# Head-wise keys spread by ScalarE and VectorE instead of by DMA, and values by half tiles, in a three-attention vision tower on one Trainium2 core

## The chip, the cores and the metric

One Trainium2 chip (trn2), one of its cores. The metric is the time of one execution on the device in microseconds, start to end. A run of the kernel is timed several times; the kernel before took 1170.06 us in the median of three runs (1166.44 to 1171.95).

## The reference

64 images of 96x96x3 are cut into 36 patches of 768 values each (2304 tokens in all) and embedded into 192 columns. Then come, all in float32:

```python
# attn1: causal attention, 12 heads of 64 columns, residual, layer norm
# attn2: attention, 12 heads of 16 columns, layer norm before it (two sizes by image),
#        no mask, no bias on q, k, v; then an MLP of 768 with gelu, mixed by gumbel weights
# attn3: attention, 12 heads of 16 columns, bias on q, k, v, ALiBi distance bias,
#        residual, layer norm after it
# moe:   top-2 of 8 experts and a shared expert of 768 columns
a = jax.nn.softmax(jnp.einsum('bhnd,bhmd->bhnm', q, k) * scale, axis=-1)
o = jnp.einsum('bhnm,bhmd->bhnd', a, v)
```

## The kernel before

The tokens stand as 18 tiles of 128 tokens. The stages run one after another: embed, `wide_stage` (attn1), `narrow_stage` (attn2), `mlp_stage`, `narrow_stage` again (attn3), `moe_stage`. Each engine has its own program, written out in order by hand, and semaphores join them; there is no planner. Between stages all engines meet at a barrier.

**Both attention stages** work in 8 groups of 288 tokens (8 images). A group has 4 units of 2 images (72 tokens), and the loop over `k` makes one step a unit, `j = k % 4`. In step k TensorE does `scores(k)`, `turn(k-2)` (transposes of the probabilities), a share of the projections for the *next* group g, `project_out` for the tiles that are ready (18 tiles in 32 units), and `mix(k-2)` (probabilities by values). Every float32 product with a weight is five matmuls of split operands (lines 286 to 290, 779 to 783). The projections of a group go to PSUM banks 0 and 1 in turn, and a bank can be written again only after what is in it has been copied out.

**wide_stage (attn1).** Twelve chunks of 128 columns a group: six of queries, then six of keys, alternating banks (`bank(c % 2)`); four of them in each of the steps j = 0, 1, 2. ScalarE copies the queries (`copy_q`, L400) and the lower half of each key chunk (`copy_k_low`, L409), VectorE the upper half (`copy_k_high`, L492), behind its `sum_up` and `take_scores` in the step. In step j = 3 come the values of the group's 2 or 3 tiles: each tile fills bank 0 and bank 1 with 384 columns each (L304 to L308), and one ScalarE copy of 768 columns (L418) empties both; the next tile's first matmul waits for it, as do the transposes of the next group's tokens (L271).

**narrow_stage (attn2, attn3).** Per group there are three chunks: c = 0 holds the queries of heads 0 to 7, c = 1 their keys, c = 2 the queries (partitions 0 to 63) and keys (64 to 127) of heads 8 to 11. The scores of all heads come out of one matmul because the keys stand block-diagonally: `keys_a[p][16h:16h+16, h, :]` has head h's keys, all else is zero (cleared once by POOL, L730). ScalarE copies c = 0, 1, 2 to `q_a`, `k_a`, `qk_b` (L911 in attn2, L913 with a bias in attn3), and SP's queue spreads them by 8 DMAs (`spread_keys_a`, L653) and 4 DMAs (`spread_keys_b`, L659) of 18 KB each:

```python
for h in range(8):
    sp.dma_start(keys_a[g % 2][16 * h:16 * h + 16, h, :], k_a[16 * h:16 * h + 16, :])
```

Step j = 0 transposes the group's tokens, j = 1 projects c = 0 and 1, j = 2 projects c = 2 and the first third of the values, j = 3 the other two thirds; `spread_values` (9 DMAs, L673) follows on SP. `scores` of a group's first unit waits for all 12 key DMAs. ScalarE's order in a step is `exponentiate(k-1)`, `copy_turned(k-2)`, the projection copies, `copy_z(k-2)`; VectorE's is `sum_up(k-1)`, `take_scores(k)`, then the norm's work and the residual. POOL raises to a power, shifts and normalises, and at the stage's start clears the key and value buffers. In attn3 SP, ScalarE and POOL also bring in and split the weights of the last stage (`side`: `load_step` after each `spread_values`, `load_down` once at k = 6, after `spread_keys_b(2)`).

Of the kernel before, what the change touches and what calls it, by code (L numbers as in the profile page):

```python
# [10 lines left out]
ALU = mybir.AluOpType  # L11
# [123 lines left out]
def wide_stage(nc, psum, ident, neg_half, name, h_tok, w_q, w_k, w_v, w_o, bias, q_bias, k_bias, out_bias):  # L135
# [30 lines left out]
    with Sems(nc, name) as S, ExitStack() as ctx:  # L166
# [41 lines left out]
        def _(sp):  # L208
            for t in range(NT):
                sp.wait_ge(S["v_copied"], t + 1)  # L210
# [55 lines left out]
        def _(pe):  # L266
            def transpose_x(g):
                if g > 0:
                    pe.wait_ge(S["v_copied"], tiles_upto(g - 1))
# [5 lines left out]
            def project(g, c):  # L275
                if c < 2:
                    pe.wait_ge(S["x_split"], g + 1)
                elif c < chunks + 2:
                    pe.wait_ge(S["q_copied"], chunks * g + c - 1)
                else:  # L280
                    pe.wait_ge(S["k_low_copied"], chunks * g + c - chunks - 1)
                    pe.wait_ge(S["k_high_copied"], chunks * g + c - chunks - 1)
                w, n = (w_q, c) if c < chunks else (w_k, c - chunks)
                cols, toks = slice(n * P, (n + 1) * P), group_cols(g)
                out = bank(c % 2)[:, 0:WIDE]
# [5 lines left out]
                                 ).then_inc(S["qk_done"], 1)  # L291

            def values(t):
                g = min(o for o in range(groups) if t < tiles_upto(o))
                if t == new_tiles(g)[0]:
                    pe.wait_ge(S["k_low_copied"], chunks * (g + 1))
                    pe.wait_ge(S["k_high_copied"], chunks * (g + 1))
                else:
                    pe.wait_ge(S["v_copied"], t)
                at = (t % RING) * P  # L300
                toks = slice(at, at + P)
                for b in range(2):
                    cols, out = slice(b * 384, (b + 1) * 384), bank(b)[:, 0:384]
# [4 lines left out]
                    last = nc.tensor.matmul(out, b_x[:, toks], w_v.b_lo[:, cols], start=False, stop=True)  # L308
                last.then_inc(S["v_done"], 1)
# [51 lines left out]
            for c in range(2 * chunks):  # L361
                project(0, c)
# [4 lines left out]
            for k in range(steps):  # L367
# [5 lines left out]
                if g < groups:  # L373
                    if j < 3:
                        for c in range(4 * j, 4 * j + 4):
                            project(g, c)
# [11 lines left out]
        def _(act):  # L388
# [7 lines left out]
            def copy_q(g, c):  # L396
                act.wait_ge(S["qk_done"], 2 * chunks * g + c + 1)
                if g >= 2:
                    act.wait_ge(S["scores_done"], per_group * (g - 1))
                nc.scalar.activation(q[g % 2][:, c, 0:WIDE], bank(c % 2)[:, 0:WIDE], ACT.Identity,  # L400
                                     bias=q_bias[:, c:c + 1], scale=1 / 8).then_inc(S["q_copied"], 1)

            def copy_k_low(g, n):
                act.wait_ge(S["qk_done"], 2 * chunks * g + chunks + n + 1)
# [45 lines left out]
            for n in range(chunks):  # L450
                copy_k_low(0, n)
# [1636 lines left out]
```

## Time and profile before

| | |
|---|---|
| median of three runs | 1170.06 us |
| the profiled execution | 1165.79 us, of which the span is 1164.0 us |
| busy: TensorE 1013.6, weight loads 925.2, VectorE 561.9, ScalarE 395.4, POOL 319.6 us | 87, 79, 48, 34, 27% of the span |
| attn1, from 56.8 to 328.2 us | 271.4 us |
| attn2, from 328.2 to 496.8 us | 168.6 us |
| attn3, from 631.1 to 804.5 us | 173.4 us |

The profile names instructions by line and engine: PE is TensorE's matmuls and PEld its weight loads, DVE is VectorE, ACT ScalarE, SPq the DMA queue of SyncE. A number behind an x counts instructions. In square brackets or behind a second bar stands the idle time of that engine just before, and what ended it; "issue" there means that the profile shows nothing that it waited for.

### The profile page before, as it was taken

How to read it: one execution, taken by the hardware profiler on the slowest of the kernel's cores; microseconds unless marked ns; L12 is line 12 of the kernel's file. 1: busy time of each engine (PE TensorE's matmuls, PEld its weight loads, DVE VectorE, ACT ScalarE, POOL GpSimd, SP SyncE). 2: the span in 40 equal slices, each digit the busy share in tenths (PEclk: the TensorE clock that was granted, in tenths of full speed). 3: DMA queues.
4: the chain of work that ended last, by engine and by line, in shares of the span. 5: the costliest groups of instructions: out<-in, count | busy, mean ns of one | idle time of the engine just before them, and what ended most of it. 6: DMA issues, size and time to landing. Idle time of an engine off the chain costs nothing. (4 is left out here: it accounts for less than half of the span.)

```text
span 1164.0 us, 21593 instructions
## 1 busy us (share of the span) xinstructions
PE 1013.6 (87%) x8306; PEld 925.2 (79%) x8306; DVE 561.9 (48%) x1489; ACT 395.4 (34%) x882; POOL 319.6 (27%) x349
## 2 busy tenths in 40 slices
PE   6879998999847999868998678976999999999997
PEld 6768888888735777758997466865999999999996
DVE  2225454555544666457331355654444454545444
ACT  1245554555413455323442344542212121111110
POOL 4424343443441222224223465663000000000000
PEclk9999999999977899879998898986999999999999
DMA  9711010101001111000000142210000000000000
GB/s 294 219 39 24 24 33 24 33 23 29 29 4 27 26 29 28 16 1 1 1 1 22 48 115 66 65 47 3 1 1 12 1 11 1 11 1 12 1 11 11
DMA packets 40757, 39.08 MB, mean 34 GB/s; under 512 B 21072, under 2 KB 32208, under 8 KB 40656
## 3 DMA queue, kind: packets, MB, share of 16 engines
q1 hardware_dynamic: 38528, 33.38, 10.3%
q10 hardware_dynamic: 2128, 4.34, 1.3%
q8 instruction: 66, 1.08, 0.4%
q14 instruction: 35, 0.29, 0.1%
HBM read 21.76 MB, written 1.77 MB: 20 GB/s over the span
## 5 line engine op out<-in xcount | busy, mean ns | idle before, releaser
L1485 ACT ACTIVATE moe_silu<-psum 128x384 f32<-128x384 f32 x108 | 53.2, 492 | 273.7 <-PE psum L76 266.3
L1389 POOL TENSOR_TENSOR moe_rstd<-moe_var_eps,neg_half 128x3 f32<-128x3 f32 x6 | 5.1, 851 | 349.5 <-DVE moe_var_eps L1584 349.5
L715 POOL TENSOR_TENSOR attn_prob<-attn_prob,attn_recip 100x432 f32<-100x432 f32 x64 | 58.3, 912 | 132.2 <-DVE attn_recip L1036 132.2
L839 PEld LDWEIGHTS psum<-attn_prob_t,attn_values 108*64 108x64 f32 x1024 | 66.6, 214 | 24.5 <-issue 10.5
L839 PE MATMUL psum<-attn_prob_t,attn_values 108*64 108x36 f32 x1024 | 74.1, 293 | 10.5 <-DMA attn_values<-attn_v_tok 6.2
L1555 DVE TENSOR_TENSOR moe_hid_pair<-psum,moe_silu 128x384 f32<-128x384 f32 x72 | 40.1, 557 | 87.3 <-PE psum L76 87.3
L813 PE MATMUL psum<-attn_keys_a,attn_q_a 128*64 128x288 f32 x256 | 51.2, 480 | 35.4 <-issue 23.2
L1571 DVE SCALAR_TENSOR_TENSOR moe_acc<-psum,moe_coef,moe_acc 128x192 f32<-128x192 f32 x144 | 59.7, 418 | 44.9 <-PE psum L1439 44.5
L1439 PE MATMUL psum<-w_dn,moe_hid_pair 128*128 128x192 f32 x288 | 73.4, 337 | 6.3 <-DVE moe_acc L1571 6.3
L72 PE MATMUL psum<-moe_x_a_hi,w_gu_a_hi 128*128 128x384 f32 x216 | 76.2, 353 | 0.0
L235 POOL TENSOR_TENSOR attn_prob_x<-attn_prob,attn_recip 100x864 f32<-100x864 f32 x32 | 52.6, 1643 | 76.4 <-DVE attn_recip L517 76.4
L74 PE MATMUL psum<-moe_x_a_hi,w_gu_a_lo 128*128 128x384 f32 x216 | 72.9, 338 | 0.0
L73 PE MATMUL psum<-moe_x_a_lo,w_gu_a_hi 128*128 128x384 f32 x216 | 72.9, 338 | 0.0
L76 PE MATMUL psum<-moe_x_b,w_gu_b_lo 128*128 128x384 f32 x216 | 72.9, 337 | 0.0
L75 PE MATMUL psum<-moe_x_b,w_gu_b_hi 128*128 128x384 f32 x216 | 72.8, 337 | 0.0
L1031 DVE TENSOR_REDUCE attn_row_sum<-attn_prob 100x12 f32<-100x432 f32 x64 | 38.5, 602 | 63.2 <-ACT attn_prob L927 62.9
L1439 PE MATMUL psum<-w_dn_mid,moe_hid_pair 128*128 128x192 f32 x288 | 69.0, 335 | 0.0
L1236 ACT ACTIVATE mlp_hid<-psum,columns 128x384 f32<-128x384 f32 x72 | 39.9, 581 | 54.2 <-PE psum L76 36.3
L1439 PEld LDWEIGHTS psum<-w_dn,moe_hid_pair 128*128 128x128 f32 x288 | 49.0, 190 | 10.9 <-DVE moe_acc L1571 10.7
L1439 PEld LDWEIGHTS psum<-w_dn_mid,moe_hid_pair 128*128 128x128 f32 x288 | 47.0, 189 | 4.9 <-DVE moe_acc L1571 3.7
L1726 PE MATMUL psum<-embed_w_tok,embed_patches 128*128 128x192 f32 x216 | 39.5, 341 | 10.3 <-DMA embed_w_tok<-in_tok_w 5.8
L1726 PEld LDWEIGHTS psum<-embed_w_tok,embed_patches 128*128 128x128 f32 x216 | 36.4, 197 | 13.1 <-DMA embed_patches<-in_x 7.2
(318 smaller groups left out, 2698.3 us busy)
## 6 DMA issues: line engine op xcount, KB each, us to landing
embed_patches<-in_x SPq DMA_DIRECT2D x18, 384.0 KB, 23.1
attn_v<-attn_v_tok SPq DMA_DIRECT2D x16, 216.0 KB
attn_values<-attn_v_tok SPq DMA_DIRECT2D x96, 27.0 KB
attn_keys_a<-attn_k_a SPq DMA_DIRECT2D x128, 18.0 KB, 1.8
raw_a<-in_w_gu_dram SPq DMA_DIRECT2D x8, 288.0 KB, 3.2
raw_b<-in_w_gu_dram SPq DMA_DIRECT2D x16, 144.0 KB, 3.2
y<-moe_y SPq DMA_DIRECT2D x6, 288.0 KB
attn_keys_b<-attn_qk_b SPq DMA_DIRECT2D x64, 18.0 KB, 1.8
```

The costliest lines, as they stand in the source:

```text
L72: nc.tensor.matmul(out, w.a_hi[:, cols], x.a_hi[:, toks], start=True, stop=False)
L73: nc.tensor.matmul(out, w.a_hi[:, cols], x.a_lo[:, toks], start=False, stop=False)
L74: nc.tensor.matmul(out, w.a_lo[:, cols], x.a_hi[:, toks], start=False, stop=False)
L75: nc.tensor.matmul(out, w.b_hi[:, cols], x.b[:, toks], start=False, stop=False)
L76: return nc.tensor.matmul(out, w.b_lo[:, cols], x.b[:, toks], start=False, stop=True)
L235: nc.gpsimd.tensor_tensor(prob_x[k % 2][:, :, :, :], prob[k % 3][:, :, :].rearrange("p h (a n) -> p h a n", a=1) .to_broadcast([QP, HEADS, ...
L715: nc.gpsimd.tensor_tensor(pr, pr, recip[k % 2][:, :].rearrange("p (h a) -> p h a", a=1) .to_broadcast([QP, HEADS, SEQ]), ALU.mult).then_in ...
L839: last = nc.tensor.matmul(ps[r:r + 64, n // 2, a * SEQ:(a + 1) * SEQ], v[:, n, :], prob_t[k % 2][:, n, a, :], start=True, stop=True)
L1439: last = nc.tensor.matmul(down_ps(n), hid(gr)[:, c, t * MT:(t + 1) * MT], w, start=(m == 0), stop=(m == len(terms) - 1))
L1485: nc.scalar.activation(silu[c % 2][:, :], bank(2 * (c % 2))[:, 0:MW], ACT.Silu).then_inc(S["silu_done"], 1)
L1571: ins = nc.vector.scalar_tensor_tensor(out=acc[:, t, :], in0=down_ps(n), scalar=scalar, in1=h_tok[:, 3 * i + t, :] if e == 0 else acc[:, t ...
L1726: last = nc.tensor.matmul(out_bank(t), patches[:, t, c, :], w_tok[:, c, :], start=(c == 0), stop=(c == chunks - 1))
```

## The change

It does four things. (1) attn1: values are handed over by half tiles: each bank has its own semaphore count and its own copy of 384 columns. (2) attn1: query and key chunks alternate, queries always in bank 0 and keys in bank 1, two pairs in each of j = 0, 1, 2; VectorE's copies follow, two in each of these steps instead of two in j = 1 and four in j = 2. (3) attn2, attn3: `spread_keys_a` and `spread_keys_b` and the buffer `k_a` are gone. ScalarE writes each head's keys straight from PSUM, eight copies of 128x288 scaled by a column of a 0/1 head mask, four behind `copy_z` in j = 1 and four in j = 2; VectorE writes the last four heads in one instruction in j = 2 (`mask_keys_b`). For the first group VectorE does both, the first as one instruction of 8x288 columns (`mask_keys_a0`). `keys_a` needs no clearing. (4) The first third of the values moves from j = 2 to j = 3 and waits for the eight masked copies, since they read bank 1. A head mask is made once at the start from the identity matrix, and a bias column by head for attn3.

```diff
@@ wide_stage, TensorE @@
-            def project(g, c):
-                if c < 2:
+            def project(g, kind, c):
+                if c == 0:
                     pe.wait_ge(S["x_split"], g + 1)
-                elif c < chunks + 2:
-                    pe.wait_ge(S["q_copied"], chunks * g + c - 1)
+                elif kind == 0:
+                    pe.wait_ge(S["q_copied"], chunks * g + c)
                 else:
-                    pe.wait_ge(S["k_low_copied"], chunks * g + c - chunks - 1)
-                    pe.wait_ge(S["k_high_copied"], chunks * g + c - chunks - 1)
+                    pe.wait_ge(S["k_low_copied"], chunks * g + c)
+                    pe.wait_ge(S["k_high_copied"], chunks * g + c)
+                out = bank(kind)[:, 0:WIDE]
...
                 for b in range(2):
+                    if t > new_tiles(g)[0]:
+                        pe.wait_ge(S["v_copied"], 2 * (t - 1) + b + 1)
+                    elif b == 0:
+                        pe.wait_ge(S["q_copied"], chunks * (g + 1))
+                    else:
+                        pe.wait_ge(S["k_low_copied"], chunks * (g + 1))
+                        pe.wait_ge(S["k_high_copied"], chunks * (g + 1))
...
@@ wide_stage, ScalarE and VectorE @@
+                for b in range(2):
+                    act.wait_ge(S["v_done"], 2 * t + b + 1)
+                    nc.scalar.activation(v_tok[t % vt_ring][:, b * 384:(b + 1) * 384], bank(b)[:, 0:384], ACT.Copy
+                                         ).then_inc(S["v_copied"], 1)
...
+                if g < groups and j < 3:
+                    copy_k_high(g, 2 * j)
+                    copy_k_high(g, 2 * j + 1)
@@ narrow_stage, SyncE @@
-            spread_keys_a(0)
-            spread_keys_b(0)
             spread_values(0)
...
-                if g < groups:
-                    if j == 1:
-                        spread_keys_a(g)
-                    if j == 2:
-                        spread_keys_b(g)
-                    if j == 3:
-                        spread_values(g)
+                if g < groups and j == 3:
+                    spread_values(g)
@@ narrow_stage, POOL @@
-                nc.gpsimd.memset(qk_b[p][:, WIDE:], 0.0).then_inc(S["pads_cleared"], 1)
+                nc.gpsimd.memset(q_b[p][:, :], 0.0).then_inc(S["pads_cleared"], 1)
             def clear(p):
-                nc.gpsimd.memset(keys_a[p][:, :, :], 0.0).then_inc(S["keys_cleared"], 1)
-                nc.gpsimd.memset(keys_b[p][:, :, :], 0.0).then_inc(S["keys_cleared"], 1)
+                nc.gpsimd.memset(keys_b[p][:, :, :], 0.0).then_inc(S["keys_b_cleared"], 1)
@@ narrow_stage, TensorE @@
             def values(g, n):
-                if n == 2:
-                    pe.wait_ge(S["v_copied"], 3 * g + 1)
-                else:
-                    pe.wait_ge(S["qk_copied"], 3 * g + 2 + n)
+                if n == 0:
+                    pe.wait_ge(S["keys_a_made"], 8 * g + 8)
+                elif n == 1:
+                    pe.wait_ge(S["q_b_copied"], g + 1)
+                    pe.wait_ge(S["keys_b_made"], g + 1)
+                else:
+                    pe.wait_ge(S["v_copied"], 3 * g + 1)
...
                         project(g, 2)
-                        values(g, 0)
                     else:
-                        values(g, 1)
-                        values(g, 2)
+                        for n in range(3):
+                            values(g, n)
@@ narrow_stage, ScalarE @@
+            def mask_keys_a(g, heads):
+                act.wait_ge(S["qk_done"], 3 * g + 2)
+                if g >= 2:
+                    act.wait_ge(S["scores_done"], per_group * (g - 1))
+                for h in heads:
+                    out, mask = keys_a[g % 2][:, h, :], head_mask[:, h:h + 1]
+                    if qk_bias is None:
+                        ins = nc.scalar.activation(out, bank(1)[:, 0:WIDE], ACT.Copy, scale=mask)
+                    else:
+                        ins = nc.scalar.activation(out, bank(1)[:, 0:WIDE], ACT.Identity,
+                                                   bias=k_bias_by_head[:, h:h + 1], scale=mask)
+                    ins.then_inc(S["keys_a_made"], 1)
...
                 if 2 <= k < units + 2:
                     copy_z(k - 2)
+                if g < groups and j == 1:
+                    mask_keys_a(g, range(4))
+                if g < groups and j == 2:
+                    mask_keys_a(g, range(4, 8))
@@ narrow_stage, VectorE @@
+            def spread_masked(out, keys, mask, bias):
+                both = [keys.rearrange("p (a n) -> p a n", a=1).to_broadcast(list(out.shape)),
+                        mask.rearrange("p (h a) -> p h a", a=1).to_broadcast(list(out.shape))]
+                if bias is None:
+                    return nc.vector.tensor_tensor(out, both[0], both[1], ALU.mult)
+                return nc.vector.scalar_tensor_tensor(out=out, in0=both[0], scalar=bias, in1=both[1],
+                                                      op0=ALU.add, op1=ALU.mult)
+
+            def mask_keys_a0():
+                dve.wait_ge(S["qk_done"], 2)
+                spread_masked(keys_a[0][:, :, :], bank(1)[:, 0:WIDE], head_mask[:, :],
+                              None if qk_bias is None else qk_bias[:, 1:2]).then_inc(S["keys_a_made"], 8)
...
             split_x(0)
+            mask_keys_a0()
+            mask_keys_b(0)
             if prenorm:
                 pre_stat(1)
                 pre_norm(1)
...
+                if j == 2 and g + 1 < groups:
+                    mask_keys_b(g + 1)
@@ prepare @@
-                    nc.vector.memset(c2_scale[0:DB, :], 0.25)
-                    nc.vector.memset(c2_scale[DB:P, :], 1.0)
-                    dve.wait_ge(S["const_ready"], 2)
+                    dve.wait_ge(S["const_ready"], 3)
+                    nc.vector.tensor_reduce(head_mask[:, :], ident[:, :].rearrange("p (h n) -> p h n", h=8),
+                                            axis=AX.X, op=ALU.add).then_inc(S["head_mask_ready"], 1)
```

## Rows read from the trace of the kernel before

**Rows 1.** Waits of PE in attn1 (56 to 327 us): total us, times, longest

```profile
PE psum L304 <- ACT attn_v_tok L418: 9.0, 10, 0.9
PE psum L286 <- DVE attn_k_diag L492: 6.4, 7, 1.1
PE psum L271 <- ACT attn_v_tok L418: 6.3, 7, 0.9
```

**Rows 2.** The same view in attn2 (327 to 496.5 us)

```profile
PE psum L813 <- issue: 7.8, 7, 1.9
```

**Rows 3.** The same view in attn3 (633 to 804 us)

```profile
PE psum L813 <- issue: 15.4, 7, 4.5
PE psum L839 <- DMA attn_values<-attn_v_tok: 6.2, 2, 5.6
PE psum L813 <- DMA attn_keys_b<-attn_qk_b: 5.9, 1, 5.9
```

**Rows 4.** ScalarE's groups of instructions in attn1: busy us, mean ns | idle before

```profile
L418 ACT ACTIVATE attn_v_tok<-psum 128x768 f32<-128x768 f32 x18 | 14.6, 810 | 32.8 <-PE psum L308 32.8
...
L393 ACT ACTIVATE attn_a_hi<-psum 128x384 fp32r<-128x384 f32 x2 | 1.0, 490 | 13.2 <-PE psum L272 13.2
```

**Rows 5.** Timeline of attn1, step j = 2: start us, duration us, engine line

```profile
221.15 0.37 PE L286 MATMUL psum<-attn_a_hi,w_k_a_hi 128*128 128x288 f32 x1 [0.88 <-DVE attn_k_diag L492]
```

**Rows 6.** Timeline of the start of attn2

```profile
332.34 5.04 DVE L998 TENSOR_SCALAR attn_x_hat<-h_tok,attn_pre_mv,attn_pre_rstd 128x192 f32<-128x192 f32 x3 [1.85 <-POOL attn_pre_rstd L704]
334.15 2.01 POOL L730 MEMSET attn_keys_a<- 128x2304 f32 x1
...
342.40 0.62 DVE L982 BATCH_NORM_STATS2 attn_pre_stats<-h_tok 128x6 f32<-128x192 f32 x2
344.33 2.12 DVE L998 TENSOR_SCALAR attn_x_hat<-h_tok,attn_pre_mv,attn_pre_rstd 128x192 f32<-128x192 f32 x2 [0.82 <-POOL attn_pre_rstd L704]
345.23 0.41 ACT L911 ACTIVATE attn_k_a<-psum 128x288 f32<-128x288 f32 x1 [0.79 <-PE psum L783]
...
354.63 1.23 PE L813 MATMUL psum<-attn_keys_a,attn_q_a 128*64 128x288 f32 x4 [6.33 <-DMA attn_keys_b<-attn_qk_b]
```

**Rows 7.** VectorE's one long operation with a broadcast operand, at the kernel's start

```profile
10.81 1.96 DVE L1734 TENSOR_TENSOR embed_pos<-embed_pos,embed_b_tok 128x1728 f32<-128x1728 f32 x1 [10.81 <-DMA embed_b_tok<-in_tok_b]
```

**Rows 8.** ScalarE's copies scaled by a column: ns min/median/max, first and last start

```profile
L911 ACT ACTIVATE attn_qk_b<-psum,c_scale x8: 500/501/501, 346.4 to 467.1; 128x288 f32<-128x288 f32 x8
L913 ACT ACTIVATE attn_qk_b<-psum,columns,c_scale x8: 583/590/593, 638.7 to 773.5; 128x288 f32<-128x288 f32 x8
```

**Rows 9.** Timeline of PE in attn3: the scores of four steps, two mixes

```profile
664.27 1.09 PE L813 MATMUL psum<-attn_keys_a,attn_q_a 128*64 128x288 f32 x4 [3.29 <-issue]
...
669.32 0.69 PE L813 MATMUL psum<-attn_keys_a,attn_q_a 128*64 128x288 f32 x4
...
672.99 0.69 PE L813 MATMUL psum<-attn_keys_a,attn_q_a 128*64 128x288 f32 x4
...
676.16 1.15 PE L839 MATMUL psum<-attn_prob_t,attn_values 108*64 108x36 f32 x16
677.13 0.69 PE L813 MATMUL psum<-attn_keys_a,attn_q_a 128*64 128x288 f32 x4
...
679.40 1.16 PE L839 MATMUL psum<-attn_prob_t,attn_values 108*64 108x36 f32 x16
```

**Rows 10.** Groups over the whole kernel: ScalarE's exponential and its copy of the transposes

```profile
L927 ACT ACTIVATE attn_prob<-attn_prob 100x432 f32<-100x432 f32 x64 | 35.7, 558 | 7.6 <-POOL attn_prob L722 7.5
...
L934 ACT ACTIVATE attn_prob_t<-psum 108x288 f32<-108x288 f32 x64 | 26.2, 409 | 58.4 <-PE psum L823 58.2
```

**Rows 11.** Timeline of SP's queue in attn3, the value DMAs of group 2

```profile
689.01 7.96 SPq L673 DMA_DIRECT2D attn_values<-attn_v_tok  x9
```

**Rows 12.** Windows without the stages' starts and ends: busy PE, PEld, DVE, ACT, POOL; clock

```profile
372.20:474.00 101.80, 94.38 (x936) 78.26 (x938) 63.31 (x159) 51.94 (x135) 25.45 (x29) 0.95 0.12 28
664.20:780.60 116.40, 98.65 (x936) 81.37 (x937) 69.65 (x176) 53.93 (x135) 69.53 (x79) 0.88 0.28 73
```

More of the change, by code:

```diff
@@ L307, in values @@
                     nc.tensor.matmul(out, b_x[:, toks], w_v.b_hi[:, cols], start=False, stop=False)
-                    last = nc.tensor.matmul(out, b_x[:, toks], w_v.b_lo[:, cols], start=False, stop=True)
-                last.then_inc(S["v_done"], 1)
+                    nc.tensor.matmul(out, b_x[:, toks], w_v.b_lo[:, cols], start=False, stop=True
+                                     ).then_inc(S["v_done"], 1)
             def scores(k):
@@ L360, in _ @@
             transpose_x(0)
-            for c in range(2 * chunks):
-                project(0, c)
+            for c in range(chunks):
+                project(0, 0, c)
+                project(0, 1, c)
             for t in new_tiles(0):
@@ L374, in _ @@
                     if j < 3:
-                        for c in range(4 * j, 4 * j + 4):
-                            project(g, c)
+                        for c in (2 * j, 2 * j + 1):
+                            project(g, 0, c)
+                            project(g, 1, c)
                     else:
@@ L449, in _ @@
                 copy_q(0, c)
-            for n in range(chunks):
-                copy_k_low(0, n)
+                copy_k_low(0, c)
             for t in new_tiles(0):
@@ L462, in _ @@
                     if j < 3:
-                        for c in range(4 * j, 4 * j + 4):
-                            if c < chunks:
-                                copy_q(g, c)
-                            else:
-                                copy_k_low(g, c - chunks)
+                        for c in (2 * j, 2 * j + 1):
+                            copy_q(g, c)
+                            copy_k_low(g, c)
                     else:
@@ L486, in copy_k_high @@
             def copy_k_high(g, n):
[L487 removed]
+                dve.wait_ge(S["k_done"], chunks * g + n + 1)
                 if g >= 2:
@@ L809, in scores @@
                 ps = scores_ps(k)
-                for q, keys, h0, h1 in ((q_a, keys_a, 0, 8), (qk_b, keys_b, 8, HEADS)):
+                for q, keys, h0, h1 in ((q_a, keys_a, 0, 8), (q_b, keys_b, 8, HEADS)):
                     for a in range(2):
@@ L949, in _ @@
             round_x(0)
-            for c in range(3):
-                copy_qk(0, c)
+            copy_q(0, 0)
+            copy_q(0, 2)
             for n in range(3):
```

112 lines of the change are left out of this document (43 added, 69 removed).

## The prediction

> **What bounds the kernel now.** I read the busy times first: TensorE is at 87% and every other engine below half, so what counts is where TensorE stands still, and I asked for its waits in each of the three attention stages. In attn1 [rows 1] the reader should see three regular waits: ten of 0.9 us for the copy of a value tile, seven of 0.9 us for the same copy ahead of the transposes, seven of about 0.9 us for VectorE's half of a key chunk. In attn2 and attn3 [rows 2, 3] the waits stand before `scores` (L813), once a group: 7.8 and 15.4 us in seven each. They are labelled "issue", but the first group of each stage waits at the same line for the last key DMA by name [rows 3, 6], and the seven are the seven other groups' first scores; I take them for the key DMAs too. One more wait, of 5.6 us, is for a group's values [rows 3]. Third, the windows: without starts and ends TensorE's granted clock is 0.95 in attn2 and 0.88 in attn3 [rows 12]. There are two levels, 1.2 and 2.4 GHz, so 0.95 means 0.10 x 101.8 = 10 us and 0.88 means 0.24 x 116.4 = 28 us at the lower one, 38 us in all.
>
> **The change part by part.**
>
> *Half tiles.* A tile's copy is 0.81 us for 768 columns, while 384 columns take 0.49 [rows 4]. Copying bank 0 now runs under the five matmuls into bank 1, which last longer than it does, so the ten waits go: -9.0. Ahead of the transposes the last half is still awaited, 0.81 - 0.49 = 0.32 shorter each, 7 x 0.32: -2.2.
>
> *Alternation.* The wait for VectorE [rows 5] falls once a group today, in j = 2, because two chunks are finished there before VectorE leaves `take_scores`. Afterwards the second key chunk of each of three steps waits for the first one's upper half. It comes third in the step, not second, so most of VectorE's delay has passed. Bounds: none (-6.4 in all) and a full 0.88 in each (7 x 3 x 0.88 = 18.5, so +12.1). I take 0.35 each, being two thirds of a microsecond later than the row's: 7 x 3 x 0.35 = 7.4 less 6.4: +1.0. attn1 together: -10.2.
>
> *Start of attn2.* POOL no longer clears `keys_a`, 2.0 us before its first power and 2.0 us behind it. The three scalings at 332.34 took 5.04 us [rows 6] and ended, at 337.38, as POOL's last memset of that run did; two such operations took 2.12 beside another memset. I read it as VectorE standing behind POOL: fewer memsets, an end 3.2 us earlier. If it were only slowed in proportion, the operations would start 1.3 us earlier and end so: -1.3, the term's other bound. The Trainium skill's page "SBUF — State Buffer", section "Who interferes with whom", states the first reading: one port pair is shared by the two engines as an exclusive lock, and the loser waits for the whole instruction.
>
> Next, the keys. The K chunk is ready at 345.2, the scores start at 354.6: 9.4 us [rows 6]. Instead VectorE writes 2304 columns. The nearest row is 1728 columns in 1.96 us [rows 7], 1.13 ns each: 2.6 us, and 1152 columns more are 1.4 (with the fixed part). The values then follow at half clock, some 2 us, for the banks are held by the masks. Scores at +5.9: 3.5 earlier. But group 1's statistics and scaling, which ran from 342.4 to 346.45 under cover [rows 6], now stand behind the masks, 4.0 us, and VectorE takes no scores before that: 345.2 + 4.0 + 4.0 = 353.2 against some 356.2 (scores 354.6 and their 1.6): 3.0 earlier. attn2's start: -6.2.
>
> *Start of attn3.* No norm there, so 3.5 of the 5.9 us [rows 3] go, less 0.5 since the 9 value DMAs (7.5 us of issue) then land late: -3.0.
>
> *Key waits, other groups.* The masked keys are there one step before the scores. -7.8 and -15.4 [rows 2, 3]: -23.2.
>
> *Values of group 2.* SP issues them at 689.01 [rows 11], behind key DMAs and ten loads of the down weights. With no key DMA between, those loads go out two steps earlier: -5.6.
>
> *What takes their place.* ScalarE gets eight copies a group. A copy scaled by a column is 0.50 us, with bias 0.59 [rows 8]; copies that follow each other overlap by some 0.1, so four are 1.6 in attn2, 2.0 in attn3. They stand behind `copy_z`, and behind them wait the exponential (0.56) and the copy of the transposes (0.41) [rows 10] that `mix` needs. From the end of one mix: `copy_z` and latency 0.3 (estimate), masks to 1.9 or 2.3, exponential and copy to about 2.85 or 3.25. Today a j = 2 step starts its mix 3.17 us after its scores (672.99 to 676.16 [rows 9]), with a tile of output projection (0.75, an estimate) and the first third of the values (0.47) in it; without the tile 2.4. Eighteen of 32 steps have a tile. So j = 2 costs on average nothing in attn2 and +0.4 in attn3. In j = 3, scores and transposes end 1.3 us after the mix (677.13 to 679.40 less two thirds of the values), and then the first third waits for the masks until 2.1 or 2.4: +0.8 or +1.1; its own 0.47 comes in; and the last third waits for the first one's copy behind the exponential: +0.25 to 0.4. Sum per group: 1.5 in attn2, 2.4 in attn3. Over seven groups each: 10.5 + 16.8 = +27.3. Bounds: masks at their full 0.50 and 0.59, with the overlap gone, raise it to about 38; masks that fit in today's gaps, ScalarE being busy only half of the time [rows 12], bring it to 6.6 (only the moved third of the values would show, 14 x 0.47).
>
> *VectorE's* 1.4 us for the last heads in j = 2 I cost at nothing: it is 63 us busy of 102 in attn2 [rows 12] and stands between `take_scores` and the next exponential. If that slack is gone it costs up to 1.4 x 14 = 20. The head mask at the start waits for an identity that POOL makes in the first microseconds, while VectorE stands idle for its first 10.81 us [rows 7]: nothing.
>
> *Clock.* The step from 664.27 to 669.32 took 5.05 us mostly at 1.2 GHz, the next, with more work, 3.67 [rows 9]: at least 0.27 us lost for each at that level, I take 0.3. Of the 38 us the waits of 3 to 5.6 us [rows 3] explain most, and those go; new ones of 1 us come. I give back a third: 38 x 0.3 / 3: -4.0. Bounds: +30 (below) and -11.4.
>
> **Sum:** -10.2 - 6.2 - 3.0 - 23.2 - 5.6 + 27.3 - 4.0 = -24.9. The profiled execution was 1165.79 with a span of 1164.0; it becomes 1140.9. It lies 4.3 below the median of the runs, 1170.06; against that median: **1145.2**. About 0.5% (5.9 us) is what a measurement of this kernel can tell from no change.
>
> **The rivals.**
>
> *attn1 gives nothing.* VectorE is late in all three steps (the +12.1 bound in place of +1.0), which eats the half tiles: 1145.2 + 11.1 = 1156. For it: VectorE leaves `take_scores` at about the same point of each step. Against: the second key chunk is one later.
>
> *ScalarE is the new pace.* Masked copies take 0.59 in both stages and do not overlap: four are 2.4, so +0.8 twice a group in attn2 and +0.4 in attn3, (1.6 + 0.8) x 7 = 17, and no clock comes back, +4: 1166. No change to speak of.
>
> *Slower: the clock falls in every group.* The long wait once a group is replaced by two or three short ones between short pieces of work, and TensorE runs at 1.2 GHz for half of each group. At 10 us in each of 14 groups it is 140 us at the lower level instead of the 25 that I expect: 115 x 0.3 = +35: 1180. It decides from about 126 us on, 9 a group (1145.2 + 101 x 0.3 = 1176). For it: the clock was down for 7 us in attn2 after waits of hardly 2 us in the longest [rows 2, 12]. Against: attn1, with waits of 0.9 us several times a group, shows no lowered clock in its steady part. The Trainium skill's page "TensorE: Matmul & The Clock Gate", section "What's actually happening", says that low is the default and activity lifts it, which would allow this.
>
> *It does not do what it says.* The waits labelled "issue" are not for keys and stay: 1145.2 + 23.2 = 1168. Against: they stand only before a group's first scores.
>
> **How the numbers follow.** Forecast 0.50, attn1 nothing 0.15, ScalarE's pace 0.16, slower 0.14, "issue" 0.05. Faster by over 0.5% are the first two and a part of the third: 0.70; within 0.5%: 0.16; slower: 0.14. The range reaches down to the forecast with the clock's whole 11.4 and no wait for VectorE (1145 - 7 - 7 = 1131) and up to the rivals at 1166 and 1168; 1168. The slower case stays out, and some of the gains beyond 1131.
>
> **What would show it.** attn1 shorter by about 10 us, no L304 wait for ScalarE, the VectorE wait three times a group at 0.3 to 0.4. attn2's first scores some 6 us earlier. No wait before `scores`; in its place one of about 1 us before the first third of the values, released by ScalarE's masked copies, and mix waiting for the copy of the transposes. SP's down loads two steps earlier and no 5.6 us wait. ScalarE's busy time up by 55 to 60 us, VectorE's by 27. A granted clock above 0.9 in both windows. I am wrong if masked copies are slower than 0.59, if the clock falls below 0.85 in the narrow stages, or if attn1 does not get shorter.

## The result, and the profile after the change

| | before | after |
|---|---|---|
| median of the runs | 1170.39 us (1166.44 to 1171.95, 4) | 1128.4 us (1125.69 to 1129.45, 4) |
| profiled execution / its span | 1165.79 / 1164.0 us | 1127.97 / 1126.2 us |

The ratio is 0.966 (95% interval 0.963 to 0.969). The forecast was 1145.2 with a range of 1131 to 1168: the direction was right, the gain 42 us where 25 had been forecast, and the result lies below the range. The whole profiled kernel:

```profile
span 1126.2 us, 21589 instructions
PE 1015.9 (90%) x8306; PEld 926.1 (82%) x8306; DVE 588.3 (52%) x1507; ACT 434.6 (39%) x996; POOL 313.2 (28%) x345
```

VectorE does 26 us more than before (forecast 27), ScalarE 39 us more (forecast 55 to 60). Next four stages, as windows of the changed kernel: attn1, attn2, mlp, attn3 (here up to the first instruction of moe). The columns are the window, its length, the busy time of TensorE, its weight loads, VectorE, ScalarE and POOL, then TensorE's granted clock, DMA share and rate.

```profile
56.80:316.80 260.00, 243.82 (x2832) 221.37 (x2832) 132.91 (x315) 136.06 (x312) 106.78 (x107) 0.97 0.11 29
316.80:473.20 156.40, 130.85 (x1244) 105.84 (x1244) 105.43 (x233) 85.34 (x228) 41.52 (x50) 0.90 0.06 13
473.20:609.80 136.60, 120.16 (x756) 117.40 (x757) 61.26 (x177) 48.57 (x85) 32.66 (x37) 0.92 0.00 1
609.80:769.10 159.30, 135.27 (x1244) 108.37 (x1245) 108.13 (x243) 93.51 (x229) 102.14 (x117) 0.89 0.21 56
```

and the same windows of the kernel before:

```profile
56.80:328.20 271.40, 239.01 (x2832) 217.71 (x2832) 133.52 (x314) 132.90 (x294) 106.71 (x106) 0.99 0.10 28
328.20:496.90 168.70, 135.42 (x1244) 110.41 (x1244) 94.88 (x225) 69.58 (x180) 45.09 (x52) 0.85 0.09 22
496.90:631.10 134.20, 117.39 (x756) 114.66 (x757) 61.12 (x177) 48.57 (x85) 32.60 (x37) 0.95 0.00 1
631.10:806.90 175.80, 138.03 (x1248) 112.53 (x1249) 94.17 (x234) 73.22 (x181) 105.12 (x119) 0.84 0.23 61
```

attn1 is 11.4 us shorter, attn2 12.3, attn3 16.5, mlp, which nobody touched, 2.4 longer at a lower clock; the run-in before attn1 and moe are the same within 0.3 us. That is the whole difference of the spans, 37.8.

TensorE's waits in attn1, attn2 and attn3 after the change (us in all, times, longest), the rows that answer to [rows 1], [rows 2] and [rows 3]:

```profile
PE psum L271 <- ACT attn_v_tok L421: 4.1, 7, 0.6
PE psum L285 <- DVE attn_k_diag L492: 1.2, 2, 0.8
```

```profile
PE psum L768 <- ACT attn_keys_a L897: 4.9, 7, 0.7
PE psum L814 <- issue: 1.7, 6, 0.8
```

```profile
PE psum L768 <- ACT attn_keys_a L899: 5.4, 5, 1.1
PE psum L814 <- issue: 4.6, 6, 1.2
PE psum L814 <- ACT attn_prob_t L920: 3.8, 4, 1.5
PE psum L814 <- DMA attn_values<-attn_v_tok: 0.7, 1, 0.7
```

No wait stands before `scores` (L788) any more: with the key DMAs the "issue" waits of 7.8 and 15.4 us [rows 2, 3] are gone. The waits are now at the first third of the values (L768), released by ScalarE's masked copies, and before `mix` (L814). The 5.6 us for a group's values are 0.7.

The start of attn2, where [rows 6] showed the scores 26.4 us after the stage's start; they are now 19.9 after it:

```profile
318.63 0.86 POOL L675 TENSOR_TENSOR attn_pre_rstd<-attn_pre_var,neg_half 128x3 f32<-128x3 f32 x1
319.43 1.80 POOL L704 MEMSET attn_values<- 108x2048 f32 x1
319.52 3.26 DVE L986 TENSOR_SCALAR attn_x_hat<-h_tok,attn_pre_mv,attn_pre_rstd 128x192 f32<-128x192 f32 x3 [0.97 <-POOL attn_pre_rstd L675]
321.33 1.05 POOL L701 MEMSET attn_keys_b<- 128x1152 f32 x1
...
330.70 2.56 DVE L1003 TENSOR_TENSOR attn_keys_a<-psum,head_mask 128x2304 f32<-128x2304 f32 x1 [2.93 <-PE psum L753]
333.29 1.36 DVE L1003 TENSOR_TENSOR attn_keys_b<-psum,head_mask 64x1152 f32<-64x1152 f32 x1
...
336.71 1.23 PE L788 MATMUL psum<-attn_keys_a,attn_q_a 128*64 128x288 f32 x4
```

The three scalings again end (322.78) just behind POOL's last memset (322.38). The masks took 2.56 and 1.36 us (estimates: 2.6 and 1.4).

Last, the steady stretches of attn2 and attn3, from the first scores to the last of each stage. Before:

```profile
354.60:484.30 129.70, 118.25 (x1128) 96.08 (x1130) 79.56 (x196) 61.93 (x161) 31.71 (x36) 0.91 0.11 27
647.00:789.50 142.50, 119.29 (x1130) 96.88 (x1131) 84.67 (x210) 66.49 (x164) 85.03 (x96) 0.89 0.26 69
```

and after:

```profile
336.70:461.60 124.90, 113.41 (x1130) 91.50 (x1130) 90.54 (x205) 78.52 (x211) 33.43 (x38) 0.98 0.08 16
622.50:752.00 129.50, 115.33 (x1129) 92.18 (x1129) 94.37 (x216) 87.70 (x214) 85.33 (x96) 0.96 0.25 64
```

From here on these are called the steady stretches. Of the two levels, 1.2 and 2.4 GHz, a clock of 0.91 over 129.7 us means 2 x 0.09 x 129.7 = 23 us at the lower one, and 0.89 over 142.5 means 31: 54 us before. After, it is 5 + 10 = 15. The amount differs between runs of the same code: e1 and e2 below have these two stages as before, and spent 59 and 48 us at the lower level in them.

**The ruler for what follows** is the length of a step, from one unit's scores to the next unit's. At the upper clock the steps of like content agree to a few hundredths of a microsecond within a trace and between kernels, so a group of four steps, without its wait, can be compared closely. Before the change a narrow group took 3.43 + 3.67 + 4.15 + 3.42 = 14.67 us (attn2, scores at 372.25, 375.68, 379.35, 383.50, 388.58, less the key wait of 1.66) and its key wait on top; after it 15.84 in attn2 (353.48 to 369.32) and 16.54 in attn3 (638.80 to 655.34). Other groups have output projections in other steps and are longer; these are the shortest.

### The profile page after: what moved, and what is told of

It reads as the page before. It is cut to its first block and busy times, and to the rows that moved or that the text cites. A ratio compares the mean times of both kernels' runs of the same rounds, so it can differ in the third digit from the quotient of the medians.

```text
span 1126.2 us, 21589 instructions
## 1 busy us (share of the span) xinstructions
PE 1015.9 (90%) x8306; PEld 926.1 (82%) x8306; DVE 588.3 (52%) x1507; ACT 434.6 (39%) x996; POOL 313.2 (28%) x345
## 5 line engine op out<-in xcount | busy, mean ns | idle before, releaser
L814 PEld LDWEIGHTS psum<-attn_prob_t,attn_values 108*64 108x64 f32 x1024 | 66.9, 214 | 26.3 <-issue 15.4
L814 PE MATMUL psum<-attn_prob_t,attn_values 108*64 108x36 f32 x1024 | 73.9, 291 | 12.6 <-issue 6.3
L1453 PEld LDWEIGHTS psum<-w_dn,moe_hid_pair 128*128 128x128 f32 x288 | 49.0, 190 | 10.9 <-DVE moe_acc L1585 10.7
L788 PE MATMUL psum<-attn_keys_a,attn_q_a 128*64 128x288 f32 x256 | 47.7, 449 | 0.0
L1740 PEld LDWEIGHTS psum<-embed_w_tok,embed_patches 128*128 128x128 f32 x216 | 39.5, 210 | 9.8 <-DMA embed_w_tok<-in_tok_w 5.7
```

The costliest lines, as they stand in the source:

```text
L814: last = nc.tensor.matmul(ps[r:r + 64, n // 2, a * SEQ:(a + 1) * SEQ], v[:, n, :], prob_t[k % 2][:, n, a, :], start=True, stop=True)
L1453: last = nc.tensor.matmul(down_ps(n), hid(gr)[:, c, t * MT:(t + 1) * MT], w, start=(m == 0), stop=(m == len(terms) - 1))
L1740: last = nc.tensor.matmul(out_bank(t), patches[:, t, c, :], w_tok[:, c, :], start=(c == 0), stop=(c == chunks - 1))
```

## The experiments

Ratios are to the kernel before, which ran beside each of them on the same chip.

### Which half of attn1's edit pays

The first kernel has the half tiles alone, the second the alternation alone, the rest is as before. The cuts show the main lines; the waits and the other engines' copies follow them.

```diff
 e1, wide_stage
-                nc.scalar.activation(v_tok..., both, ACT.Copy).then_inc(S["v_copied"], 1)
+                for b in range(2):
+                    act.wait_ge(S["v_done"], 2 * t + b + 1)
+                    nc.scalar.activation(v_tok[t % vt_ring][:, b * 384:(b + 1) * 384], bank(b)[:, 0:384], ACT.Copy
+                                         ).then_inc(S["v_copied"], 1)
 e2, wide_stage
-                        for c in range(4 * j, 4 * j + 4):
-                            project(g, c)
+                        for c in (2 * j, 2 * j + 1):
+                            project(g, 0, c)
+                            project(g, 1, c)
```

> The kernel before with the half tiles alone (values and their copies by 384 columns; query and key chunks in the old order). Theory A (the sum's term): the ten waits of 0.9 us go and the transposes wait 0.32 us less in each of seven groups, -11.2 us, about 1159 (ratio 0.990 to 0.991); the wait for VectorE's key halves stays at 6.4 us in seven. Rival B (the waits as the list of waits has them, of which 5.2 us went with VectorE's): with the old order only about half of attn1's gain comes, -6, about 1164 (0.995).

> The kernel before with the alternation alone (query and key chunks in turn, VectorE's halves two a step; whole value tiles and their copies in one). Theory A, from the lengths of the steps after the change (one projection step a group 0.65 us shorter, the two others 0.26 and 0.28 us longer): nothing, -1 us, within 0.998 to 1.002, though the list of waits shows VectorE's wait for key halves at 1 to 2 us in place of 6.4. Rival B, from the list of waits: -5 us, ratio 0.9955. Rival C, the forecast's upper bound: +12 (1.010).

Measured: half tiles 0.9904 (0.9873 to 0.9935), alternation 1.0027 (0.9998 to 1.0056). Theory A holds for the first. The second comes out just above the 1.002 that A allowed: no gain, and perhaps a small cost. Rivals B and C are out for it. One full group of attn1, step by step, in the four traces (us):

| | 1st | 2nd | 3rd | 4th, with the values | group |
|---|---|---|---|---|---|
| before | 7.62 | 5.68 | 8.55 | 9.03 | 30.88 |
| half tiles | 7.63 | 5.66 | 8.55 | 7.61 | 29.45 |
| alternation | 7.88 | 5.93 | 7.89 | 9.20 | 30.90 |
| both | 7.88 | 5.94 | 7.90 | 7.60 | 29.32 |

The list of waits reads quite differently. Alternation alone:

```profile
PE psum L285 <- DVE attn_k_diag L491: 1.2, 2, 0.8
```

VectorE's wait fell from 6.4 us [rows 1] to 1.2, and the stage gained nothing: it lasted 274.4 us, where it had been 271.4. Where the 5.2 us went is in the changed kernel's timeline, at the second key chunk of a step:

```profile
135.44 0.29 PE L289 MATMUL psum<-attn_b_x,w_q_b_lo 128*128 128x288 f32 x1
135.80 0.37 PE L285 MATMUL psum<-attn_a_hi,w_k_a_hi 128*128 128x288 f32 x1
```

Matmuls of this kind follow each other 0.13 us apart; here it is 0.36. Of the 0.23 us more, only 0.07 stand in the trace as idle time, between the end of the one matmul (135.73) and the start of the next (135.80), so the list does not name them.

### The narrow stages by themselves

```diff
 e3: narrow_stage and its callers as changed, wide_stage as before
```

> The changed narrow stages with the first stage as before. Theory A (the parts add): -26 to -31 us, about 1140 (ratio 0.974 to 0.978), with attn2 and attn3 as in the changed kernel: first scores 6.5 us earlier, steady granted clock 0.99 and 0.96 in place of 0.94 and 0.89, groups at full clock 15.84 and 16.54 us long. Rival B (the clock of attn2 and attn3 depends on what attn1 does before them): the steady granted clock stays at 0.94 or 0.89 in one of them, and 5 us less are gained (0.979 or more).

Measured: 0.9799 (0.9765 to 0.9833), a span of 1137.5, 26.5 less than before. The ratio alone does not choose: it lies a little above what A gave, and its interval (-20 to -27 us) takes in both theories. The trace does. Groups at full clock are 15.83 and 16.56 us, the granted clock over the steady stretches 0.96 in both stages (0.98 and 0.96 in the changed kernel, 0.91 and 0.89 before), and their lengths are 126.2 and 130.0 us against 124.9 and 129.5. The clock that came back in the narrow stages did not come from attn1's change.

### Is the wait for values a wait for the down weights?

```diff
 e4: before, SyncE
-                if side and k == per_group + 2:
+                if side and k == 2 * per_group:
                     side.load_down(sp)
```

> The kernel before, with the loads of the down weights on SyncE two steps later, behind the values of group 2. Keys stay on DMAs. Theory A: the wait of 5.6 us for group 2's values goes, and with it the step behind it runs at the full clock: -5.6 and some -2 to -3 for the clock, ratio 0.992 to 0.994; the granted clock of the 18 us with that wait rises from 0.81 to 0.95 or more. Rival B: the loads then stand in the way of group 3's keys or values, and the wait only moves: within 0.998 to 1.001. Rival C: the wait goes, the clock does not come back: -5.6 (0.995).

Measured: 1.0019 (0.9989 to 1.0049): rival B. The values' wait is gone, and the next one for keys is 9.3 us, and all of them together 21.5 us in place of 15.4 [rows 3] (in all, times, longest):

```profile
PE psum L813 <- issue: 21.5, 7, 9.3
```

SyncE's queue shows why (start, time in all, DMAs):

```profile
682.76 7.50 SPq L673 DMA_DIRECT2D attn_values<-attn_v_tok  x9
690.30 0.52 SPq L1800 DMA_DIRECT2D raw_a<-in_w_gu_dram  x1
690.86 1.18 SPq L1802 DMA_DIRECT2D raw_b<-in_w_gu_dram  x2
692.08 0.59 SPq L1783 DMA_DIRECT2D w_dn_shared<-in_ws_down  x1
692.72 0.54 SPq L1785 DMA_DIRECT2D w_dn<-in_w_down  x1
693.30 7.82 SPq L1790 DMA_DIRECT2D w_dn_mid<-in_w_down  x8
701.22 5.00 SPq L653 DMA_DIRECT2D attn_keys_a<-attn_k_a  x8
706.27 2.48 SPq L659 DMA_DIRECT2D attn_keys_b<-attn_qk_b  x4
```

A group's DMAs occupy SyncE for 5.0 + 2.5 + 7.5 + 1.7 = 16.7 us of the 17 to 18 that a group lasts. Wherever ten more loads (9 us) are put, they land on somebody. The change takes the 7.5 us of key DMAs off this queue. The loads then start 1.7 us behind the third step's scores (647.61 against 645.88), where it had been 8.0 (680.96 against 672.99), with the values' DMAs behind them. That this room in the queue, and nothing else, removed the 5.6 us is the reading; no run took the key DMAs away alone.

### Does the clock follow the stalls?

To the changed kernel, one tiny DMA a group (e5) or two in a chain (e6), issued when a mix is done, for which the third step's scores wait (the cut shows e5; e6 issues a second DMA when the first has landed and waits for both):

```diff
 e5: SyncE
+                if j == 2 and k < units and k > 2:
+                    sp.wait_ge(S["mixed"], k - 2)
+                    sp.dma_start(lag[:, :], q_a[0][0:16, WIDE:WIDE + 8]).then_inc(S["lag"], 16)
 TensorE, scores(k)
+                if u == 2 and k > 2:
+                    pe.wait_ge(S["lag"], 16 * g)
```

> The changed kernel, and in both narrow stages TensorE waits before the third step's scores of groups 1 to 7 for one tiny DMA (16 x 8 elements of zeros into a tile that nobody reads) that SyncE issues when the mix before is done: 14 stalls of about 2.2 us (estimate: issue 0.6 and landing under 2). Theory A (the clock follows TensorE's stalls: before, stalls of 1.6 to 1.9 us were followed by steps at 1.2 GHz in about half of the cases, of 3.3 us and more always, each such spell some 2.5 us lost): the stalls, 28 to 34 us, and 14 to 20 on top of them, granted clock of the steady stretches 0.99 and 0.96 down to about 0.92 and 0.90; ratio to the kernel before 1.003 to 1.012. Rival B (the clock came back for another reason): the stalls alone, 28 to 34 us, clock as it was; ratio 0.990 to 0.995.

> The same with two such DMAs one behind the other, so 14 stalls of about 4.4 us, 62 us in all. Theory A: each is followed by a spell at 1.2 GHz, 2.5 to 3 us lost in each, +35 to +42 on top of the stalls; steady granted clock 0.80 to 0.87; ratio 1.050 to 1.056. Rival B: the stalls alone, +62; ratio 1.019 to 1.022.

Measured: 1.0151 (1.0088 to 1.0214) and 1.0422 (1.0359 to 1.0485). The stalls were longer than estimated, above all in attn3. The short stalls in attn2 and attn3, and the steady stretches around them:

```profile
PE psum L798 <- DMA attn_lag<-attn_q_a: 13.5, 7, 2.3
PE psum L798 <- DMA attn_lag<-attn_q_a: 28.6, 7, 4.8
338.20:486.30 148.10, 125.23 (x1130) 99.67 (x1130) 91.86 (x205) 79.99 (x211) 34.25 (x39) 0.87 0.07 13
649.20:814.20 165.00, 126.52 (x1131) 99.66 (x1132) 95.30 (x218) 90.02 (x214) 87.29 (x98) 0.86 0.19 50
```

and the long ones:

```profile
PE psum L798 <- DMA attn_lag<-attn_q_a: 25.0, 7, 3.8
PE psum L798 <- DMA attn_lag<-attn_q_a: 39.5, 7, 6.3
340.20:501.10 160.90, 126.60 (x1130) 100.21 (x1130) 92.23 (x205) 80.11 (x211) 33.52 (x38) 0.86 0.06 12
664.60:843.20 178.60, 129.57 (x1129) 102.45 (x1129) 95.38 (x218) 90.27 (x214) 87.36 (x98) 0.82 0.18 46
```

The span of e5 is 62.3 us above the changed kernel's with 42.1 us of stalls, that of e6 89.9 with 64.5: 20 and 25 us beyond the stalls, against none in rival B; of these, 17 and 21 lie in the steady stretches (148.1 + 165.0 - 124.9 - 129.5 - 42.1 = 16.6). So the clock does follow them, and in kind theory A is right: 2 x 0.13 x 148 + 2 x 0.14 x 165 = 85 us at 1.2 GHz in e5, where the changed kernel has 15, and 109 us in e6. Each microsecond more at the lower level cost 0.24 us in e5 and 0.22 in e6 by the steady stretches, 0.29 and 0.27 by the spans. Its price was wrong for the longer stalls: e5 lies in the expected +14 to +20, e6 far below +35 to +42. A stall beyond its own length cost 1.2 to 1.4 us in e5 and 1.5 to 1.8 in e6, not 2.5 to 3. Each of the seven stalls of 1.8 to 2.3 us in e5's attn2 was followed by a spell at 1.2 GHz (the steps behind them have clocks of 0.50 to 0.75). It is no sharp rule: in the kernel before, a wait of 1.9 us (372.25) was followed by none. In the changed kernel, whose waits in the steady groups are mostly 0.7 to 1.2 us, no such spell follows them in attn2 between 349 and 461 us; in attn3 two spells follow waits of 1.3 and 1.2 us before `mix` (steps at 633.23 and 684.25, clocks 0.71 and 0.73), and the second of them is missing when the same kernel is run again (e9).

### What the new waits consist of

```diff
 e7: ScalarE, mask_keys_a
                 for h in heads:
+                    if g >= 2 and h != heads[-1]:
+                        continue
```

> The changed kernel without six of ScalarE's eight masked key copies in each group from group 2 on, in both narrow stages (those keys keep what group 0 or 1 left there); everything else, the third of the values that moved included, stays. Theory A (what took the place of the key waits are ScalarE's masks): the waits before the values, 0.70 and 1.07 us a group, and those before the mix of the third step, 0.17 and 0.54, go: -0.8 x 6 in attn2, -1.5 x 6 in attn3, -14 us, ratio 0.954 (0.951 to 0.957). Rival B (it is the moved third of the values and VectorE's masks): -3 us at most, 0.963 to 0.966.

From the third group on this kernel leaves out six of the eight masked copies. Measured: 0.9571 (0.9502 to 0.9639), 1119.2 us. The interval is wide, but the group at the upper clock can be read closely: 14.64 us in attn2 and 14.62 in attn3, where the group before took 14.67 without its key wait. In these groups all of the 1.17 and 1.87 us by which the changed one is longer is ScalarE's masks; VectorE's mask and the moved third of the values cost nothing. Over six groups the same holds in attn2: 93.1 us against 99.3, 1.0 a group, with 3.4 us at the lower clock on e7's side alone. It does not hold in attn3: 98.2 against 103.7, 0.9 a group and not 1.87. Without the masks other waits show there, before `mix` and before the transposes of the probabilities, 10.1 us in all, where the kernel before had 5.0 besides the 5.6 for the values. The wait before the values is listed once in attn2 in place of seven times, in group 1, which still has its masks:

```profile
PE psum L768 <- ACT attn_keys_a L899: 0.7, 1, 0.7
```

### Towards a better version

Two remedies for those waits. e8 gives the first third of the values other columns to land in, so that it needn't wait for the last mask; `mix` in the fourth step waits for their copy instead. e10 uses ScalarE's idle time: in the changed kernel it stands still before it copies z, and only then begins the four masks, with the next exponential behind them.

```profile
364.69 0.29 ACT L930 ACTIVATE attn_z_t<-psum 128x144 f32<-128x144 f32 x1 [1.03 <-PE psum L814]
364.88 1.67 ACT L897 ACTIVATE attn_keys_a<-psum,head_mask 128x288 f32<-128x288 f32 x4
366.41 0.59 ACT L913 ACTIVATE attn_prob<-attn_prob 100x432 f32<-100x432 f32 x1
```

```diff
 e8: values(g, n)
-                out = bank((n + 1) % 2)[0:m, 0:D]
+                out = (bank(6)[:, 2 * UNIT:2 * UNIT + D], bank(0)[:, 0:D], bank(1)[:, 0:D])[n][0:m, :]
 e10: ScalarE; early is 2, but 0 where j == 1 and side is given
+                    mask_keys_a(g, range(4 * j - 4, 4 * j - 4 + early))
                     copy_z(k - 2)
+                    mask_keys_a(g, range(4 * j - 4 + early, 4 * j))
 e11: both of them
 e12: e11, and two early masks and the rounding of expert weights in other steps of attn3
-                if side and j == 1 and g <= groups:
+                if side and j == 0 and g <= groups:
```

> A try at a better version: in the narrow stages the first third of the values goes to the free columns 288 to 479 of the bank that mix writes, the second to bank 0 and the last to bank 1, so that no third waits for the last masked copy, and mix in the fourth step waits for the copy of the first third. Theory: the waits before the values go (0.70 and 1.07), but mix then waits for exponential, transposes and first third copied one behind the other after the masks: 0.4 us a group gained in attn2 and 0.35 in attn3, -5 us, ratio 0.9615 (0.958 to 0.965). Rival: ScalarE's chain is what sets the end of this step already, nothing gained, 0.966.

> The changed kernel itself, beside the three that follow: ratio 0.966 (0.963 to 0.969).

> The changed kernel, but of the four masked copies of a step two come ahead of the copy of z (in both steps of attn2, in the third step alone in attn3, where the rounding of the expert weights fills the gap of the second). ScalarE stands idle there for 0.9 to 1.3 us until the mix is done, and two copies take 0.84 to 1.0. Theory (the masks cost what they delay behind the copy of z): the wait before the values, 0.70, goes in attn2 and most of 1.07 in attn3; group at full clock 15.84 to 15.0 in attn2, 16.54 to 15.6 in attn3, -12 us against the changed kernel, ratio 0.956 (0.953 to 0.960). Rival (the copy of z and with it the output projection get later by as much): nothing, 0.966.

> The two early masks and the values' first third in the spare columns together. Theory: attn2's group falls to 14.7, as without masks (14.64), attn3's to 15.0: -18 us against the changed kernel, ratio 0.951 (0.947 to 0.955). Rival: the early masks have taken all that the spare columns gave, 0.956.

> The same, and in attn3 ScalarE rounds the expert weights in the first step of a group, not the second, so that the second step has the gap for two early masks as well. Theory: attn3's group 15.0 to 14.8, -1 to -2 us more, ratio 0.949. Rival: the rounding comes before its data has landed or delays the rounding of x, a new wait of 0.5 us or more a group, +3 us, 0.954.

| | ratio (95% interval) | median us | group, attn2 | group, attn3 | steady attn2 | steady attn3 |
|---|---|---|---|---|---|---|
| changed kernel again, e9 | 0.9639 (0.9623 to 0.9655) | 1127.3 | 15.84 | 16.54 | 125.3 | 129.7 |
| spare columns, e8 | 0.9618 (0.9559 to 0.9676) | 1122.0 | 15.20 | 15.78 | 122.1 | 129.5 |
| two masks early, e10 | 0.9581 (0.9565 to 0.9597) | 1120.6 | 14.81 | 15.78 | 118.2 | 129.5 |
| both, e11 | 0.9595 (0.9577 to 0.9613) | 1121.2 | 14.48 | 15.69 | 117.7 | 129.9 |
| rounding moved too, e12 | 0.9573 (0.9549 to 0.9596) | 1119.2 | 14.48 | 14.64 | 117.6 | 126.7 |

e8 was measured beside another set of runs of the kernel before than the four others. Its ratio is what its theory said (0.9615), but partly by luck: the span is 6.8 us shorter than the changed kernel's, of which the steady attn2 has 2.8 (0.4 a group had been expected), attn3 0.1 (0.35 a group expected), and 3.1 lie between attn2's last scores and attn3's first, where mlp stands, which it leaves alone. e10, a move of two calls, beats both kernels: its interval lies below the changed kernel's. It is inside the range of its theory (0.953 to 0.960), with less gain than the middle of it. In attn2 it gave 7.1 us, where 0.84 a group had been expected; ScalarE there now reads

```profile
362.40 0.87 ACT L897 ACTIVATE attn_keys_a<-psum,head_mask 128x288 f32<-128x288 f32 x2
363.83 0.29 ACT L930 ACTIVATE attn_z_t<-psum 128x144 f32<-128x144 f32 x1 [0.56 <-PE psum L814]
364.02 0.89 ACT L897 ACTIVATE attn_keys_a<-psum,head_mask 128x288 f32<-128x288 f32 x2
364.79 0.57 ACT L913 ACTIVATE attn_prob<-attn_prob 100x432 f32<-100x432 f32 x1
```

In attn3 it gave nothing (129.5 against 129.7), though the group at full clock is 0.76 shorter and some 6 us had been expected: the wait before the values' first third is gone from the list, and the waits before `mix` and before the transposes (L798) have grown:

```profile
PE psum L814 <- ACT attn_prob_t L920: 5.3, 7, 1.5
PE psum L814 <- issue: 5.2, 6, 1.3
PE psum L798 <- POOL attn_prob L686: 2.5, 3, 1.4
```

Those rows add up to 13.0 us against 10.0 in the changed kernel (4.6 + 3.8, and 1.6 for POOL). The first steps of later groups grew too: those at 647.29 and 699.07 took 3.83 and 5.38 us, where the changed kernel's (655.34 and 707.27) took 3.41 and 4.54. So something else than the masks sets the pace of most groups in attn3. The rows name ScalarE, POOL and, as "issue", nothing; which link it is was not separated. e11 and e12 missed their theories (0.951 and 0.949): the spare columns add nothing measurable once two masks are early, as the rival had it, and e12's group in attn3 is 1.1 us shorter than e10's, but the whole stretch only 2.8, and the two intervals overlap.

## Why the prediction was wrong

The mechanisms were right and two sizes were not. From first to last scores attn2 and attn3 became 4.8 and 12.9 us shorter, together 17.7, where the terms for them (-23.2 - 5.6 + 27.3 - 4.0) gave 5.5: nearly the whole miss of 12.9 us lies there. Term by term, in spans (forecast, measured):

| term | forecast | measured | from |
|---|---|---|---|
| attn1 | -10.2 | -11.4 | stage windows |
| attn2, start to first scores | -6.2 | -6.5 | 26.4 to 19.9 |
| attn3, start to first scores | -3.0 | -3.2 | 15.9 to 12.7 |
| key waits of the other groups | -23.2 | -23.2 | none left at `scores` |
| values of group 2 | -5.6 | -4.9 | 0.7 left |
| what takes their place | +27.3 | +21.3 | 7 x 1.17 + 7 x 1.87, groups at the upper clock |
| clock, steady stretches | -4.0 | -10.9 | remainder of 4.8 and 12.9 us, below |
| ends of the stages, mlp, moe | none | +1.1 | stage windows |
| sum | -24.9 | -37.8 | the spans |

**The step that failed first is "I give back a third".** In the steady stretches the terms for the waits make -7.8 + 8.2 = +0.4 in attn2 and -15.4 - 4.9 + 13.1 = -7.2 in attn3, and what remains of 4.8 and 12.9 is 5.2 + 5.7 = 10.9 us. Time at 1.2 GHz fell by 39 us there, so 0.28 us came back for each: close to the price of 0.3, and to the 0.22 to 0.29 that e5 and e6 give without any such sum. The stock was 54 us and not 38, as the windows read for [rows 12] had left out the ends of the stretches, and 39 of them went, not 13. That 10.9 lies so near the lower bound of -11.4 is luck: the bound was all of a stock that was too small. The 10.9 is a remainder and good to a few microseconds only. In attn2 e7 bears it out; in attn3 the 13.1 is one group's 1.87 taken seven times, and e7's 0.9 a group says that up to half of it is not the masks but other waits. I had argued that the new waits of 1 us would hold most of the clock down. e5 and e6 show that stalls of 1.8 us and more do this, fourteen of them taking back 17 to 20 us; the changed kernel's shorter ones did not in attn2, and in attn3 at most twice. The range had taken the clock's bound and attn1's together (1131) and nothing from the new waits, whose 6 us put the result outside.

**The second is the sum per group of the new waits, 1.5 and 2.4, where 1.17 and 1.87 came.** By step: the third was to cost nothing and +0.4 and cost -0.27 and +0.09 (4.15 to 3.88, 4.15 to 4.24); the fourth was to cost 1.5 and 2.0 and cost 1.44 and 1.79 (3.42 to 4.86 and 5.22). A third of the values that moves from one step to the next is no added work, as e7's 14.64 against 14.67 says; the account charged it in full to the step that took it, and credited the step that gave it up only in part. The lower bound of 6.6, which was that third alone, was no bound.

**attn1** came out at 11.4 for 10.2. The half tiles carry it: 1.42 us in the step with values, e1's 0.9904 is 11.2 us of 1169, which is the forecast's 9.0 + 2.2. For the alternation the forecast took 0.35 us in each of three steps against 0.92 saved in one; the steps say 0.26, 0.25 and -0.66, and 0.17 more in the fourth step as long as the tiles are whole: nothing in sum. Here the list of waits would have misled: read as it stands, it credits VectorE's rows with 5.2 us.

**The starts** were right to 0.3 us each. In attn2 the scalings began 1.4 us earlier in the stage and took 3.26 us instead of 5.04, so they ended 3.2 earlier, as forecast, and in both kernels they ended with POOL's last memset. The Trainium skill's page "SBUF — State Buffer", section "Who interferes with whom", says that the engine which comes second on the shared pair waits for the whole instruction of the first. The two traces agree with that in the main: before the change, the 18 scalings took 0.37 us in the median, and the first of them 1.82 us beside a memset of 1.80, the second 2.19 beside one of 2.01, ending 0.11 us behind each. No run here took POOL's work away alone.

**The rivals.** "attn1 gives nothing" fell with e1; "ScalarE is the new pace" was right about who makes the new waits (e7) and wrong about the amount; "it does not do what it says" fell with the list of waits; the slower case was wrong for the changed kernel and is what e6 looks like: 109 us of the steady stretches at 1.2 GHz (2 x 0.14 x 160.9 + 2 x 0.18 x 178.6). The masks' place was not thought through: four in a row behind the copy of z, with 1.0 us idle ahead of it, is why they cost more than 0.14 us a group in attn2 (e10's 14.81 against 14.67).

## What to carry to other kernels

A stall of TensorE is not its length alone: price the wait together with the spell at the lower clock behind it. When waits of some microseconds go, most of the time at the lower level can go with them (39 of 54 us here), at 0.2 to 0.3 us of gain for each. To size a change, compare like steps at the upper clock between two traces, since delays of 0.2 us need not be in any list of waits, and moved work is not added work. A step that is shorter in one group is not yet shorter in all: count the groups. Before putting new work behind a wait on an engine, look for the idle time ahead of that wait.

## What was not expected of the hardware

- Stalls of 1.8 to 2.3 us, once every 19 to 20 us, each brought a spell at 1.2 GHz (0.87 over attn2's steady stretch in e5, 0.98 without them). Stalls of 3.5 to 3.8 us in the same place (e6) cost hardly more beyond their own length: 11.0 us for seven (160.9 - 124.9 - 25.0) against 9.7 (148.1 - 124.9 - 13.5).
- Masked copies that follow each other on ScalarE take 1.67 us for four, 0.42 each, where one alone is listed with 0.50; with bias 2.03, 0.51 each against 0.59. That is why its busy time grew by 39 us and not by 55 to 60.
- SyncE needs 0.62 us for each of the small key DMAs and 0.83 for those of the values, 16.7 us a group: a queue that issues can be full while the DMA engines are a quarter busy (0.26 in the steady attn3 before).
